# Adapters and retention layer as one program, with two of the four key products behind the turn of the first pair of rows

## The reference, cut to what matters

```
x = x + L1_ffn(layernorm(x))
x = x + L2_xattn(layernorm(x), ctx, ctx)

def L1_ffn(x, Wr, br, Wd, bd, Wu, bu):             # 8 adapters of rank 16, top 2
    gates = softmax(x @ Wr + br + bonus)
    w = top two of gates, divided by their sum, zero elsewhere
    h = relu(x @ Wd[e] + bd)
    out = sum over e of w[e] * (h[e] @ Wu[e] + bu[e])

def L2_xattn(x, k, v, Wh, wg_w, wo_w, gn_gamma, gn_beta):   # 2 heads of 128
    Q, K, V = x, k, v, each times Wh per head
    scores = Q K^T / sqrt(128)                     # 128 x 128 per head and sequence
    masked = scores * Dn                           # Dn: decay mask
    A = maximum(abs(masked.sum over the sequences), 1)
    O = A applied to V
    Y = (O - mean) / sqrt(var + 0.001) * gn_gamma + gn_beta
    out = (relu(x @ wg_w) * Y) @ wo_w
```

## Time and profile before

| | us |
|---|---|
| median of 3 runs | 1685.47 (1683.97 to 1686.34) |
| profiled execution, its own time | 1687.65 |
| its span, first to last instruction | 1685.8 |
| adapters, from their first DVE instruction | 1119.06 |
| retention layer, from its first matmul | 1168.97 |
| ternary layer, from its first DVE instruction | 1228.58 |
| layer 3, from its first DVE instruction | 1290.24 |

### The profile page before, as it was taken

One profiled execution on the slowest core, in us unless ns is written; L12 is line 12 of the kernel. 1 busy time (PEld: TensorE's weight loads), 2 busy tenths in 40 slices (PEclk: granted clock), 3 DMA queues, 4 the chain that ended last, 5 costly groups with the idle time before them and its releaser, 6 DMA issues. The chain is left out here.

```text
span 1685.8 us, 22398 instructions
## 1 busy us (share of the span) xinstructions
PE 1517.5 (90%) x6976; PEld 1055.1 (63%) x6976; DVE 931.3 (55%) x2063; ACT 738.5 (44%) x2055; POOL 519.9 (31%) x496
## 2 busy tenths in 40 slices
PE   3989998989969999998999999988745999999998
PEld 1667776777754555567788797753523666664555
DVE  7787988888844423223535445533676555553321
ACT  3778787788841111102344353421323555553110
POOL 2566568777640000002343342210000333320000
PEclk9999999999979999999999999976867999999999
DMA  4201000200026000001000000022020000000000
GB/s 181 96 15 57 4 4 1 77 1 1 2 73 293 0 1 0 0 0 57 1 1 1 1 1 26 1 94 83 41 101 2 1 1 1 1 1 1 0 13 13
DMA packets 9749, 52.76 MB, mean 31 GB/s; under 512 B 1813, under 2 KB 3877, under 8 KB 6560
## 3 DMA queue, kind: packets, MB, share of 16 engines
q1 hardware_dynamic: 9040, 50.50, 7.8%
q0 software_dynamic: 160, 0.68, 0.2%
q10 hardware_dynamic: 432, 0.15, 0.0%
HBM read 50.94 MB, written 1.05 MB: 31 GB/s over the span
## 5 line engine op out<-in xcount | busy, mean ns | idle before, releaser
L1204 DVE TENSOR_TENSOR l0f_hidden<-l0f_product,bank 128x512 f32<-128x512 f32 x48 | 33.0, 687 | 155.3 <-PE bank L1040 155.3
L1089 ACT ACTIVATE l0f_silu<-bank 128x512 f32<-128x512 f32 x48 | 28.7, 597 | 202.8 <-PE bank L1029 202.8
L769 POOL TENSOR_TENSOR l0a_stepped<-l0a_y,l0a_m 128x512 f32<-128x512 bf16 x64 | 76.2, 1191 | 107.5 <-DVE l0a_m L571 107.2
L791 POOL TENSOR_TENSOR l0a_head_rstd<-l0a_head_var,all_minus_half 128x4 f32<-128x4 f32 x96 | 101.0, 1056 | 13.8 <-DVE l0a_head_var L590 13.7
L2081 PE MATMUL bank<-l3a_f_xn_t,all_weights_b 128*128 128x512 f32 (+1 forms) x208 | 94.0, 594 | 1.7 <-DVE all_weights_a L2264 1.7
L722 ACT ACTIVATE l0a_work<-bank,l0a_neg_max 128x128 f32<-128x128 f32 x256 | 90.2, 368 | 6.8 <-DVE l0a_neg_max L603 6.6
L1029 PE MATMUL bank<-l0f_xn_t,all_weights_b 128*128 128x512 f32 x192 | 91.7, 600 | 0.0
L442 PE MATMUL bank<-all_ident,l0a_work 128*128 128x128 f32 x384 | 61.4, 283 | 33.6 <-DVE l0a_work L598 32.5
L1566 DVE TENSOR_TENSOR all_weights_a<-bank,all_cols 128x512 f32<-128x512 f32 x64 | 44.1, 690 | 85.8 <-PE bank L1423 85.6
L1051 PE MATMUL bank<-all_weights_a,l0f_hidden 128*128 128x256 f32 x384 | 90.5, 378 | 0.0
L1029 PE MATMUL bank<-l0f_xn_t,all_weights_a 128*128 128x512 f32 x192 | 90.2, 592 | 0.0
(11 more groups left out here) (405 smaller groups left out, 3871.0 us busy)
## 6 DMA issues: line engine op xcount, KB each, us to landing
all_weights_a<-in_l_w_q SPq DMA_DIRECT2D x2, 2048.0 KB, 15.0
all_weights_b<-in_l_e_gate SPq DMA_DIRECT2D x1, 3072.0 KB, 10.2
all_weights_a<-in_l_e_up SPq DMA_DIRECT2D x4, 768.0 KB, 9.2
all_weights_a<-in_l_e_down SPq DMA_DIRECT2D x1, 3072.0 KB, 17.9
all_weights_b<-in_l_w_qx SPq DMA_DIRECT2D x1, 2048.0 KB
all_weights_b<-in_l_w_proj_x SPq DMA_DIRECT2D x1, 2048.0 KB, 17.5
all_weights_b<-in_l_w_proj SPq DMA_DIRECT2D x1, 2048.0 KB, 8.8
all_weights_b<-in_l_w_q SPq DMA_DIRECT2D x1, 2048.0 KB
```

Source lines behind the costliest of these rows:

```text
L769: done = g.tensor_tensor(stepped[:, 0:n], value, step, ALU.add)
L791: g.tensor_tensor(head_rstd[:, m % 2, :], head_var[:, m % 2, :], res.minus_half[:, 0:HU], ALU.pow)\
```

## The change

Both programs become one, `adapters_and_retention`, with its large buffers laid into the two weight regions. The core of the diff:

```diff
-        v.bn_aggr(res.new_moments[:, i, :], res.stats[:, i, :])
-    v.drain()
-    n = len(tiles)
-    v.tensor_copy(res.moments[:, bass.ds(tiles[0], n), :], res.new_moments[:, 0:n, :])
+        v.bn_aggr(res.moments[:, t, :], res.stats[:, i, :])
     v.drain()
...
-def layer1_adapters(nc, top, res, w, ternary, before):
-def layer2_retention(nc, top, res, w, ternary, before):
+def adapters_and_retention(nc, top, res, w, ternary, loads):
...
+        @block.tensor
+            f_turn(0)
+            f_turn(1)
+            for p in range(PAIRS):
+                route(p)
+                if p + 2 < PAIRS:
+                    f_turn(p + 2)
+            for h in range(HALVES):
+                down(h)
...
+            for n in range(2):
+                keys_and_values(n)
+            turn_weights()
...
+            for h in range(HALVES):
+                spread_weights(h)
+            for p in range(PAIRS):
+                up(p)                      # waits for f_x_done >= p - 1 where p >= 2
+            ternary.add_partitions(pe, score_bank)
+            turn_rows(0)
+            keys_and_values(2)             # waits for ternary.mean_ready
+            keys_and_values(3)
+            queries(0)
+            gates_of(0)
+            turn_rows(1)
+            scores(0)
+            turn_rows(2)
+            queries(1)
+            gates_of(1)
+            turn_rows(3)
+            scores(1)
+            keys_and_values(4)
+            queries(2)
+            gates_of(2)
+            scores(2)
+            queries(3)
+            keys_and_values(5)
+            scores(3)
+            gates_of(3)
+            keys_and_values(6)
+            keys_and_values(7)
+            for p in range(PAIRS):
+                mix(p)
+            turn(0)
+            for p in range(PAIRS):
+                if p + 1 < PAIRS:
+                    turn(p + 1)
+                project_out(p)
...
+        @block.scalar
+            for h in range(HALVES):
+                act.wait_ge(weight_turned, h + 1)
+                act.activation(weight_t[0:E, h, :], pair_banks[h][0:E, :], ACT.Copy).then_inc(weight_t_ready, 1)
+            ternary.sum_squares(act, squares)
...
+            norm_mix(0)                    # two 128x256: Identity, scale=rstd, bias=offset
+            for p in range(PAIRS):
+                if p + 1 < PAIRS:
+                    norm_mix(p + 1)
+                shift(p)                   # two 128x256: Identity, scale=gamma, bias=beta
...
+        @block.vector
+            for p in range(PAIRS + 1):
+                if p < PAIRS:
+                    add_pair(p)            # add to x, token_moments, eps
+                if p >= 1:
+                    token_rows(p - 1)      # rows of the pair, behind POOL's power
+                if p == 1:
+                    ternary.mean_square(v, score_bank)   # waits for add_partitions
+            ternary.root(v)
+            ternary.round(v, squares, 0)
+            ternary.round(v, squares, 1)
+            v.wait_ge(res.loaded["l2_decay"], 16)
+            v.wait_ge(scored, 1)
...
+            for p in range(PAIRS):
+                mix_moments(p)             # bn_stats x2 from PSUM, bn_aggr x2, -mean, var + eps
+            open_gate(0)                   # one 128x512 product with the gates
+            for p in range(PAIRS):
+                if p + 1 < PAIRS:
+                    open_gate(p + 1)
+                add_to_x(p)                # one 128x512 add, token_moments of two tiles
...
+        @block.gpsimd
+                g.tensor_tensor(f_rstd[:, half], f_var[:, half], res.minus_half[:, half], ALU.pow).then_inc(f_rstd_ready, 1)
...
+                g.tensor_tensor(rstd[:, pair], var[:, pair], res.minus_half[:, pair], ALU.pow)
+                g.drain()
+                g.tensor_tensor(offset[:, pair], neg_mean[:, pair], rstd[:, pair], ALU.mult)\
+                 .then_inc(rstd_ready, 1)
...
-                layer1_adapters(nc, top, res, w, ternary,
-                                loader(res, w, "l2_w1", "l2_w2", "l2_heads", "l2_ctx_t", "l2_gate", "l2_out", "l2_decay"))
-                layer2_retention(nc, top, res, w, ternary,
-                                 loader(res, w, "l3_e_gate", "l3_e_up", "l3_route", "l3_e_down"))
-                layer2_ternary(nc, top, res, w, ternary, loader(res, w, "l3_w_q", "l3_w_o"))
+                adapters_and_retention(nc, top, res, w, ternary,
+                                       loader(res, w, "l2_heads", "l2_ctx_t", "l2_w1", "l2_w2", "l2_gate", "l2_decay", "l2_out"))
+                layer2_ternary(nc, top, res, w, ternary, loader(res, w, "l3_w_q", "l3_e_down", "l3_route", "l3_e_gate", "l3_e_up", "l3_w_o"))
```

More of the change, by code:

```diff
@@ L2464, in layer1_adapters @@
[L2464 to L2473, removed]
@@ L2474, in layer1_adapters @@
-        block = mem.ctx.enter_context(nc.Block())
-        @block.sync
-        def _(sp):
-            sp.dma_start(select[0:E, :], w["l1f_select"][0:E, :]).then_inc(small_in, 16)
-            sp.dma_start(up_bias[0:E, :], w["l1_f_bu"]).then_inc(small_in, 16)
-            sp.dma_start(route_bias[:], w["L1_ffn_br"].broadcast_to([P, E])).then_inc(small_in, 16)
[L2481 to L2544, removed]
@@ new lines, in down, with keys_and_values @@
+            def down(h):
+                if h == 0:
+                    pe.wait_ge(res.loaded["l1_f_down"], 16)
+                for c in range(KC):
+                    mm = pe.matmul(wide_banks[h][:], w_down[:, c, :], f_xn_t[:, c, h * HALF:(h + 1) * HALF],
+                                   start=(c == 0), stop=(c == KC - 1))
+                mm.then_inc(down_made, 1)
+            def keys_and_values(n):
+                kind, h, half = kv[n]
+                if n == 4:
+                    pe.wait_ge(f_x_done, PAIRS)
+                if n == 2:
+                    pe.wait_ge(ternary.mean_ready, 1)
+                    pe.wait_ge(gate.shifted, 1)
+                if n >= 6:
+                    pe.wait_ge(kv_kept, n - 1)
+                bank = kv_bank(n)
@@ L2620, in product @@
                 else:
-                    src = ctx_t if kind == "k" else xn_t
-                    mm = pe.matmul(bank[:], w_heads[:, h, :], src[:, h, half * HALF:(half + 1) * HALF],
+                    mm = pe.matmul(bank[:], w_heads[:, h, :], ctx_t[:, h, half * HALF:(half + 1) * HALF],
                                    start=True, stop=True)
-                mm.then_inc(made, 1)
-            ternary.add_partitions(pe, res.banks[7])
-            for n in range(8):
-                product(n)
@@ new lines, in turn_rows, with queries @@
+            def turn_rows(p):
+                pe.wait_ge(rows_ready, p + 1)
+                if p < 2:
+                    pe.wait_ge(hidden_done, 2)
+                else:
+                    pe.wait_ge(xn_ready, p - 1)
+                turn_pair(pair_banks[p % 2], rows, p).then_inc(rows_turned, 1)
+            def queries(p):
+                pe.wait_ge(xn_ready, p + 1)
+                if p < 2:
+                    pe.wait_ge(relu_done, 2)
+                else:
+                    pe.wait_ge(q_kept, p - 1)
+                for h in range(2):
+                    mm = pe.matmul(wide_banks[p % 2][:, h * WIDE:(h + 1) * WIDE], w_heads[:, h, :],
+                                   xn_t[:, h, p * WIDE:(p + 1) * WIDE], start=True, stop=True)
+                mm.then_inc(q_made, 1)
@@ new lines, in scores @@
+            def scores(p):
+                pe.wait_ge(q_kept, p + 1)
+                for h in range(2):
+                    for t in (2 * p, 2 * p + 1):
+                        mm = pe.matmul(score_bank[:, h * P:(h + 1) * P], k_t[:, h, t * P:(t + 1) * P],
+                                       q_t[:, h, t * P:(t + 1) * P], start=(h == 0 and t == 0),
+                                       stop=(t == TILES - 1), skip_group_check=True)
+                if p == PAIRS - 1:
+                    mm.then_inc(scored, 1)
@@ new lines, in mix, with turn @@
+            def mix(p):
+                if p == 0:
+                    pe.wait_ge(mask_ready, 1)
+                    pe.wait_ge(xn_ready, PAIRS)
+                if p % 2 == 0:
+                    pe.wait_ge(kv_kept, 6 + p)
+                for h in range(2):
+                    mm = pe.matmul(pair_view(mix_banks[p])[:, :, h, :], mask[:, h, :],
+                                   values[:, h, p * WIDE:(p + 1) * WIDE], start=True, stop=True)
+                mm.then_inc(mix_made, 1)
+            def turn(p):
+                pe.wait_ge(mix_normed, p + 1)
+                if p >= 2:
+                    pe.wait_ge(shifted, p - 1)
+                else:
+                    pe.wait_ge(kv_kept, 8)
+                for c in range(KC):
+                    for i in range(2):
+                        at = (c * 2 + i) * P
+                        mm = pe.transpose(turn_banks[p % 2][:, at:at + P], mixed[:, 2 * p + i, c * P:(c + 1) * P], res.ident[:])
+                mm.then_inc(turned, 1)
```

(29 more changed lines are left out.)

398 lines of the change are left out of this document (240 added, 158 removed), and 2 rows, old and new, of the table VECTORS.

## The result

The changed kernel takes 1661.02 us (median of 4 runs, 1660.2 to 1662.2) against 1685.57: a ratio of 0.9856, 95% interval 0.9839 to 0.9873, 24.5 us faster. The forecast was 1666.5, range 1653 to 1678. The profiled execution took 1660.2, its span 1658.4.

What follows compares the result with a forecast made beforehand. A chain of hand-overs, PE its longest link and partly at 1.2 GHz, bounds the stretch. Gains of 19.1 and 1.0 less 1.1 make 19.0: 1687.65 becomes 1668.65, less 2.18 for the median 1666.5 us; range 1653 to 1678.

Steps and rivals of the forecast that it cites:

- the 1.1 allowed for hand-overs: Over the whole sum: 1.1 us taken off the gain for hand-overs that a sum of means leaves out.
- Logits and gate: Adapters: halved POOL power ends logits 2.0 us earlier, gate unchanged at 6.97; two keys hidden in its shadow or 0.3 late.
- Turned weights: Between gate and up products: turning by halves makes 6.0 us about 3.4, so up products start 4.4 us earlier.
- Up products: Adapters: the same sixteen matmuls stay at the low clock, 1.15 us start to start, ending at 1160.8.
- a spacing under 0.7 us: Sign of being wrong: up products coming closer than 0.7 us from start to start.
- The rival of fast up products: Adapters: up products keep the high clock and end 10 us earlier; whole kernel 1655 us, chance 0.18.
- The new wait: DVE's mean_square waits for PE behind all up products; last rows at 1168.5, wanted at about 1173, so it costs nothing.
- The seam: Adapters to retention: PE works on from the up products, first mix at 1185.7 in place of 1198.32.
- The tail: From the mix to the last moments: end at 1208.6 in place of 1227.66, the tail giving 6.4 us of this.
- Copies: Copies of the moments, 0.24 us each, dropped everywhere: 1.0 us gained on the path, nothing in the middle of loops.
- Loads: 9 MB of loads now start with the ternary layer: 21 us, in time for layer 3, costing nothing.
- Beside POOL: DVE rows beside added POOL work: no slowdown taken; the skill's lock rule would make it some 2 to 4 us more.

Runs made afterwards that it cites:

- experiment 5: Changed kernel with four or no key products ahead of the up products, in place of two: 1664.02 us with four, 1669.67 with none.
- the second profile: The changed kernel run again with nothing changed, profiled once more: 1660.11 us, ratio 0.9849.
- experiments 6 and 8: 6: changed kernel with a key or value product behind each pair of up products, 1656.27 us; 8: also spare tail matmuls and a key before the spread, 1649.94.
- Experiment 2: Changed kernel with DVE's mean_square moved behind the last pair's add: 1661.70 us, ratio 0.9844.
- Experiment 4: Changed kernel with PE made to wait behind add_partitions for the last pair of normalised rows: 1666.45 us, ratio 0.9885.
- experiment 1: Kernel before without the copies of the moments: 1680.36 us, ratio 0.9960; changed kernel with them put back: 1666.12, ratio 0.9884.

## Why the prediction was right

The mechanism held, the size was 5.5 us short. In the profiles the stretch from the first variance to the last moments fell from 108.6 to 82.8 us, 25.8 in place of the 19.1 predicted: 4.8 before the first up product (predicted 4.4), 2.1 in the up products (0), 10.1 from their end to the mix (8.2) and 8.8 in the tail (6.4). Another 1.0 was predicted ahead of the stretch and 3.7 found; the 1.1 allowed for hand-overs wasn't needed. 1.9 us went the other way, in the two layers behind.

*Logits and gate.* Gate at 12.5 behind V (12.7 predicted); its end, where PE begins to turn the weights, at 19.6 (19.7). The first rows started 1.29 us behind the variance (1.3). Both keys hid, with 0.57 us of PE's wait left: experiment 5 shows that two more keys found no room: the turn came 1.7 to 1.9 us later.

*Turned weights.* Up products from 22.9 (23.3). No experiment undid the earlier logits or the halves, so these 4.8 us rest on the profile alone.

*Up products.* I took all sixteen at 1.15 us. In the profile after, the first four (eight records) went at 0.63, and all ended at 39.4, not 41.7; in the second profile it was one, and 41.1. The prediction had named a spacing under 0.7 us as a sign of being wrong; for these few it was there. Where in the sixteen the clock falls differs between executions, so that part of the miss is luck. The rival of fast up products didn't come true, but experiments 6 and 8 show it was there to be had. The low level costs what the rows said.

*The new wait.* DVE waited 6.98 us for add_partitions, as predicted, with its last rows at 1161.7 and PE asking for them at 1165.71. That it costs nothing the profile shows: PE is busy 22.60 of 22.60 us behind it, with no wait for rows. Experiment 2, which was to show it, put in a wait of its own.

*The seam.* Mix predicted at 66.6, found at 62.3 and 64.1. From the end of the up products it took 22.9 and 23.0 us, not 24.9: the two keys 2.6 and 2.7, for which 3.1 and 0.3 of hand-overs were counted, the three turns 0.44 each, not 0.6, and scores and values a little less than their rows. The clock rose 3.1 and 3.3 us behind the up products (42 to 44 behind V), not 5 (47). Experiment 4 prices the overlap: 5.4 to 6.3 of the 10.1 us.

*The tail.* Predicted 22.9 us, measured 20.5. The 10.7 us that I gave for the pairs count four turns where three were left; the end that I took, 1206.0 to 1206.5, counts three. POOL's unknown product took 0.20, once 0.41 (I took 0.5 between 0.2 and 0.8), the power 0.70; ACT's Identity 0.51 each (0.48). DVE's moments took 1.3 a pair, not 1.5. One low spell came, and cost the first projection 1.5 us (3.41 against 1.9); I had allowed 2.3. That no experiment undid the pairing of tiles leaves the rest of the 8.8 us that the tail lost against the earlier trace rows argued only: experiment 1's kernel, where the copies are gone and nothing else is, needs 27.5, so at most 1.8 of the 8.8 are the copies'.

*Copies.* This step failed: "those in the middle of loops lie beside a busy PE: nothing". I took 1.0 in all ahead of the stretch; it was 3.7 in the profile, 3.1 of it in layer 0's attention, and over the whole kernel some 6 by experiment 1. In layer 0's attention PE is busy 426 of 495 us and no engine is the bound alone; without nine copies on DVE it was shorter. Which hand-overs the copies held up wasn't followed.

*Loads.* Ternary layer 1.2 us longer, 62.9 twice against 61.7, layer 3 0.7 longer and 0.4 shorter. The kernels of experiments 2 and 6, with the changed loads, had 61.6; that of experiment 1, with the loads of before, had 62.7. So it isn't the loads. The layer's last two groups of products fell into a low spell of the clock in the profile after (0.50 from 1256.8 to 1260.2) and into a high one before:

```profile
1286.15 1.03 PE L2836 MATMUL bank<-all_ternary,l2f_mid_t 128*128 128x256 bf16 x8
1287.85 1.03 PE L2836 MATMUL bank<-all_ternary,l2f_mid_t 128*128 128x256 bf16 x8 [0.67 <-DVE all_x L2923]
...
1256.74 1.86 PE L3008 MATMUL bank<-all_ternary,l2f_mid_t 128*128 128x256 bf16 x8
1259.26 1.47 PE L3008 MATMUL bank<-all_ternary,l2f_mid_t 128*128 128x256 bf16 x8 [0.67 <-DVE all_x L3095]
```

That is 1.27 us, the whole difference. In the thirteen profiles of this case the layer took 62.7 us or more where such a spell lay over these products, and 61.6 or 61.7 where none did.

*Beside POOL.* The first eight rows took 2.68 us with POOL's second power beside them (1115.63 to 1117.77). No lock, again: the Trainium skill's rule (SBUF — State Buffer, "SBUF: two separate sides") would have made them later.

## What to carry to other kernels

Read the granted clock beside the busy time: a stretch in which PE is 100% busy can run at half the clock, so that up to half of its time can still be won, and here independent products were worth most spread over the gaps of a stretch in which the clock falls, not in one block ahead of it or behind it. A high busy share of PE doesn't make another engine's work free; take a small operation out of a loop alone and time it. Take two profiles of one kernel before a difference of 2 us between two kernels is explained, and look in an experiment's own profile for a wait that its edit put in, as in experiments 2 and 5.

## What the runs showed of the hardware

The up products, half of which use eight rows of the array, ran at 0.50 for 18.4 us in the kernel before and for 17 in the second profile of the changed one, at a busy share of 100%; with a key or value product behind every four of them the clock rose after 7 us, and with a key in the gap ahead of them too it didn't fall in the one profile taken. Layer 1's attention took 345.8 and 344.4 us in two profiles of one program. It begins at the low level, and the clock rose 6.0 us behind its first variance in the first profile and 3.1 in the second; the same stretch in both:

```profile
773.50:775.50 2.00, 2.00 (x7) 1.55 (x6) 1.35 (x4) 0.00 (x0) 0.00 (x0) 0.50 0.99 426
773.50:775.50 2.00, 2.00 (x11) 1.77 (x10) 1.82 (x6) 0.00 (x0) 0.00 (x0) 1.00 1.01 434
```

All three profiles with 346 us have the late rise, the ten with 344 the early one.
